# The search for the kept scores of an MoE layer: 16-bit keys in two halves, expert as innermost index

## What is computed

```python
c = einsum('bct,bcd->bdt', x, weights[ids])             # a 32x32 mix per sample
logits = c @ Wg + bg                                     # 4 experts
top_vals, top_idx = top_k(logits, 2); probs = softmax(over the two)
for i in range(4):                                       # capacity = 4096 / 4 = 1024
    score = where(expert i is one of the two, probs[:, i], -inf)
    sel_p, sel_idx = top_k(score, 1024)                  # the kept scores
    y = gelu(c[sel_idx] @ W1[i]) @ W2[i] * p
    out = out.at[sel_idx].add(y)
x = x + out
x = x + ffn(lora_swiglu(x, per-sample adapters))         # second layer
```

## Time and profile before

| | us |
|---|---|
| median of 3 runs | 598.33 |
| lowest, highest | 596.82, 598.34 |
| profiled execution, its own time | 598.46 |
| span of the profile | 596.7 |
| TensorE busy | 569.3 |
| VectorE busy | 380.8 |
| ScalarE busy | 241.0 |
| GpSimd busy | 142.1 |

### The profile page before, as it was taken

One profiled execution on the slowest core, in us unless ns is written; L12 is line 12 of the kernel. 1 busy time (PEld: TensorE's weight loads), 2 busy tenths in 40 slices (PEclk: granted clock), 3 DMA queues, 4 the chain that ended last, 5 costly groups with the idle time before them and its releaser, 6 DMA issues.

```text
span 596.7 us, 10231 instructions
## 1 busy us (share of the span) xinstructions
PE 569.3 (95%) x3548; PEld 474.1 (79%) x3548; DVE 380.8 (64%) x847; ACT 241.0 (40%) x545; POOL 142.1 (24%) x120
## 2 busy tenths in 40 slices
PE   4777899999999999999999999999999999999996
PEld 2656699999999999987878878778788788787885
DVE  6888767875776566656566564575565655744733
ACT  2643347666864754644412422322324033123110
POOL 3000223752563460756003002030030030100000
PEclk9998899999999999999999999999999999999999
DMA  8999579353348331643004105022041041130012
GB/s 301 321 319 291 163 231 332 53 160 74 36 125 282 36 55 18 147 102 88 1 0 131 20 3 137 13 91 55 6 125 24 0 132 18 36 83 8 9 28 35
DMA packets 64653, 61.05 MB, mean 102 GB/s; under 512 B 37504, under 2 KB 56704, under 8 KB 63264
## 3 DMA queue, kind: packets, MB, share of 16 engines
q1 hardware_dynamic: 53168, 37.99, 21.5%
q0 software_dynamic: 9264, 22.22, 15.5%
q10 hardware_dynamic: 2176, 0.26, 0.3%
HBM read 45.19 MB, written 19.47 MB: 108 GB/s over the span
## 4 chain that ended last, share of the span: by engine, by line
PE 88%; DVE 7%; DMA 2%; issue 1%; ACT 1%; SPq 1%; DVEq 0%; ACTq 0%; POOLq 0%
PE bank L1282 25%; PE bank L1283 24%; PE bank L1284 24%; PE bank L1538 5%; PE bank L1496 2%; DMA xT<-in_xT 2%; DVE passed L887 2%; PE bank L1403 1%; PE bank L1488 1%; PE bank L1392 1%; PE bank L1363 1%; PE bank L1505 1%; PE bank L1506 1%; PE bank L1626 1%; PE bank L1586 1%
## 5 line engine op out<-in xcount | busy, mean ns | idle before, releaser
L730 ACT ACTIVATE act<-bank 128x512 f32<-128x512 f32 x64 | 38.2, 599 | 181.4 <-PE bank L1538 181.4
L1238 DVE TENSOR_TENSOR prod<-bank,act 128x512 f32<-128x512 f32 x64 | 44.2, 691 | 93.3 <-PE bank L1538 75.8
L1098 DVE TENSOR_TENSOR hid_lo<-hf,hid_hi 128x512 fp32r<-128x512 f32 (+1 forms) x80 | 46.7, 585 | 51.3 <-ACT hf L660 46.8
L1282 PE MATMUL bank<-w_hi,hid_hi 128*128 128x256 f32 x256 | 71.9, 281 | 0.2 <-DVE hid_lo L1098 0.2
L1283 PE MATMUL bank<-w_lo,hid_hi 128*128 128x256 f32 x256 | 71.4, 279 | 0.0
L1284 PE MATMUL bank<-w_hi,hid_lo 128*128 128x256 f32 x256 | 71.3, 279 | 0.0
L657 ACT ACTIVATE hid_hi<-bank 128x512 fp32r<-128x512 f32 (+1 forms) x80 | 41.1, 514 | 66.1 <-PE bank L1284 59.9
L489 POOL DMA_INDIRECT x_rows<-y_sb,slot_row x32 | 54.5, 1704 | 44.3 <-ACT y_sb L629 33.6
L478 POOL DMA_INDIRECT xg<-flat_rows,slot_row x32 | 34.6, 1082 | 118.5 <-DVE slot_row L953 75.2
L1282 PE MATMUL bank<-xs_hi,w_hi 128*128 128x512 f32 (+1 forms) x160 | 57.5, 360 | 0.1
L508 POOL DMA_INDIRECT b_pair<-b_rows,b_row x8 | 8.3, 1038 | 201.8 <-PE bank L1586 201.2
(11 more groups left out here) (299 smaller groups left out, 1269.5 us busy)
## 6 DMA issues: line engine op xcount, KB each, us to landing
w_raw<-in_L_ffn_W SPq DMA_DIRECT2D x8, 1024.0 KB
flat_rows<-x_sb SPq DMA_DIRECT2D x8, 520.0 KB, 7.2
xT<-in_xT SPq DMA_DIRECT2D x8, 512.0 KB, 8.6
x_sb<-in_x SPq DMA_DIRECT2D x8, 512.0 KB, 8.7
outT<-out_sb SPq DMA_DIRECT2D x120, 32.0 KB
wdT<-in_wdT SPq DMA_DIRECT2D x1, 1024.0 KB, 5.9
wg_lo_raw<-in_L_cond_Wg SPq DMA_DIRECT2D x1, 1024.0 KB, 8.2
wu_lo_raw<-in_L_cond_Wu SPq DMA_DIRECT2D x1, 1024.0 KB
```

The lines of the kernel that those rows point to most:

```text
L730: act.activation(act1[h % 2][:, :], bank[h % 2][:, :], ACT.Silu).then_inc(silu1, 1)
L1098: dve.tensor_tensor(lo[:, n], hf[s % 2][:, n], hi[:, n].bitcast(f32), ALU.subtract).then_inc(hid0, 1)
L1238: dve.tensor_tensor(prod[par][h][:, :], bank[2 + h % 2][:, :], act1[h % 2][:, :], ALU.mult).then_inc(prod1, 1)
L1282: pe.matmul(out, lh, rh, start=start, stop=False, skip_group_check=True)
```

## The change

The pattern is searched in two halves. `high_key` is the score's bits above the lowest 15, `low_key` the lowest 15. In steps 0 to 4 the 16-bit `key` is `high_key`, less 100 for an unused expert; in steps 5 to 9 it is (high_key - found) x 2^15 + low_key, cut to 0 and 2^15 - 1, so that scores outside the found high part compare as all or nothing. Candidates are sums in place of or-ed patterns, the table of step values is fp32 and moves from `pack_i` to `pack_f2`. `key`, `cand` and `passed` have the expert as innermost index. The fp32 `score` is still made, behind the comparisons of step 0, and the threshold is put together from both halves at the end.

```diff
@@ -21,6 +21,7 @@
+HIGH_STEPS, LOW_BITS = 5, 15
@@ -34,8 +35,8 @@
-           "scale": D, "out_bias": KD}
-I_COLS = {"subj": G, "sample": TOK // 32, "steps": SEARCH_STEPS * CAND}
+           "scale": D, "out_bias": KD, "steps": HIGH_STEPS * CAND}
+I_COLS = {"subj": G, "sample": TOK // 32}
@@ -53,15 +54,15 @@
-        "steps": np.broadcast_to(np.concatenate([np.arange(1, CAND + 1, dtype=np.int32) << (SEARCH_BITS * (SEARCH_STEPS - 1 - i))
-                                                 for i in range(SEARCH_STEPS)]), (P, CAND * SEARCH_STEPS)),
+        "steps": np.broadcast_to(np.concatenate([np.arange(1, CAND + 1) * 2.0 ** (SEARCH_BITS * (HIGH_STEPS - 1 - i))
+                                                 for i in range(HIGH_STEPS)]).astype(np.float32), (P, CAND * HIGH_STEPS)),
         "behind": np.broadcast_to(np.repeat(np.arange(E - 1, -1, -1, dtype=np.float32), G), (P, E * G)),
     }
 
 
 def adaln_moe_lora(nc, A, outT):
     f32, f32r, bf16 = mybir.dt.float32, mybir.dt.float32r, mybir.dt.bfloat16
-    i32, u32 = mybir.dt.int32, mybir.dt.uint32
+    i32, u32, i16 = mybir.dt.int32, mybir.dt.uint32, mybir.dt.int16
@@ -107,7 +108,7 @@
-        steps = vi["steps"].bitcast(u32).rearrange("p (i j) -> p i j", j=CAND)
+        steps = vf2["steps"].rearrange("p (i j) -> p i j", j=CAND)
@@ -219,10 +220,12 @@
-        cand = sb("cand", [P, E, CAND], f32)
-        passed = sb("passed", [P, E, CAND, G], bf16)
+        key, cand = sb("key", [P, G, E], i16), sb("cand", [P, CAND, E], i16)
+        passed = sb("passed", [P, CAND, G, E], bf16)
         passed_n = sb("passed_n", [P, E, CAND], f32)
-        kept = [sb(f"kept{i}", [P, E, CAND + 1], f32) for i in range(2)]
+        kept = [[sb(f"kept{i}{j}", [P, E, CAND + 1], f32) for j in range(2)] for i in range(2)]
+        high_key, low_key = sb("high_key", [P, E, G], i32), sb("low_key", [P, E, G], i32)
+        key_f = sb("key_f", [P, 2, G, E], f32)
@@ -233,6 +236,8 @@
+        thr_high, thr_bits = sb("thr_high", [P, E], i32), sb("thr_bits", [P, E], i32)
+        thr = sb("thr", [P, E], f32)
@@ -340,7 +345,7 @@
-        IDLE_STEPS = [2, 2, 2, 2, 2, 4, 8, 8, 8, 8]
+        IDLE_STEPS = [2, 2, 2, 2, 2, 2, 6, 6, 6, 6]
@@ -802,7 +807,8 @@
-            dve.memset(kept[0][:, :, CAND], 0.0)
+            dve.memset(kept[0][0][:, :, CAND], 0.0)
+            dve.memset(kept[1][HIGH_STEPS % 2][:, :, CAND], 0.0)
@@ -875,17 +881,31 @@
-            link(dve.tensor_tensor(score[:, :, :], prob[:, :, :], unused[:, :, :], ALU.subtract))
-
-            counts = bank[7][:, 0:E * CAND * SUMS].rearrange("p (e j g) -> p e j g", e=E, j=CAND)
+            by_e = lambda t: t.rearrange("p e g -> p g e")
+            link(dve.tensor_scalar(high_key[:, :, :].bitcast(u32), prob[:, :, :].bitcast(u32), LOW_BITS, None, ALU.logical_shift_right))
+            dve.tensor_scalar(low_key[:, :, :].bitcast(u32), prob[:, :, :].bitcast(u32), 2 ** LOW_BITS - 1, None, ALU.bitwise_and)
+            link(dve.scalar_tensor_tensor(key[:, :, :], by_e(unused[:, :, :]), -100.0, by_e(high_key[:, :, :]), ALU.mult, ALU.add))
+
+            counts = bank[7][:, 0:E * CAND * SUMS].rearrange("p (j g e) -> p e j g", e=E, j=CAND)
             for i in range(SEARCH_STEPS):
-                now, then = kept[i % 2], kept[(i + 1) % 2]
-                link(dve.tensor_tensor(cand[:, :, :].bitcast(u32), over(now[:, :, CAND].bitcast(u32), CAND),
-                                       steps[:, i, :].unsqueeze(1).to_broadcast([P, E, CAND]), ALU.bitwise_or))
+                high = i < HIGH_STEPS
+                now, then = kept[not high][i % 2], kept[not high][(i + 1) % 2]
+                step = steps[:, i % HIGH_STEPS, :]
+                if i == HIGH_STEPS:
+                    found = kept[0][HIGH_STEPS % 2][:, :, CAND]
+                    link(dve.tensor_tensor(key_f[:, 0, :, :], key[:, :, :], found.unsqueeze(1).to_broadcast([P, G, E]), ALU.subtract))
+                    link(dve.scalar_tensor_tensor(key_f[:, 1, :, :], key_f[:, 0, :, :], 2.0 ** LOW_BITS, by_e(low_key[:, :, :]),
+                                                  ALU.mult, ALU.add))
+                    done(dve.tensor_scalar(key[:, :, :], key_f[:, 1, :, :], 0.0, 2.0 ** LOW_BITS - 1, ALU.max, ALU.min))
+                link(dve.tensor_tensor(cand[:, :, :], now[:, :, CAND].unsqueeze(1).to_broadcast([P, CAND, E]), over(step, E), ALU.add))
                 for g in ASKED:
                     n = g.stop - g.start
-                    dve.tensor_tensor(passed[:, :, :, g], score[:, :, g].unsqueeze(2).to_broadcast([P, E, CAND, n]),
-                                      over(cand[:, :, :], n), ALU.is_ge).then_inc(asked, 1)
+                    dve.tensor_tensor(passed[:, :, g, :], key[:, g, :].unsqueeze(1).to_broadcast([P, CAND, n, E]),
+                                      cand[:, :, :].unsqueeze(2).to_broadcast([P, CAND, n, E]), ALU.is_ge).then_inc(asked, 1)
+                if i == 0:
+                    done(dve.tensor_tensor(score[:, :, :], prob[:, :, :], unused[:, :, :], ALU.subtract))
+                if i == HIGH_STEPS:
+                    done(dve.tensor_scalar(thr_high[:, :], found, 2.0 ** LOW_BITS, None, ALU.mult))
@@ -897,11 +917,14 @@
-                link(dve.scalar_tensor_tensor(now[:, :, 0:CAND], passed_n[:, :, :], float(CAP), cand[:, :, :], ALU.is_ge, ALU.mult))
-                link(dve.tensor_reduce(then[:, :, CAND], now[:, :, :], AX.X, ALU.max))
-            thr = kept[SEARCH_STEPS % 2][:, :, CAND]
-
-            thr_b = over(thr, G)
+                link(dve.scalar_tensor_tensor(now[:, :, 0:CAND], passed_n[:, :, :], float(CAP), cand[:, :, :].rearrange("p j e -> p e j"),
+                                              ALU.is_ge, ALU.mult))
+                if i < SEARCH_STEPS - 1:
+                    link(dve.tensor_reduce(then[:, :, CAND], now[:, :, :], AX.X, ALU.max))
+            link(dve.tensor_reduce(thr_bits[:, :], now[:, :, :], AX.X, ALU.max))
+            link(dve.tensor_tensor(thr[:, :].bitcast(i32), thr_high[:, :], thr_bits[:, :], ALU.bitwise_or))
+
+            thr_b = over(thr[:, :], G)
@@ -1361,7 +1384,7 @@
-                                         passed[:, :, :, g].rearrange("p e j g -> p (e j) g"),
+                                         passed[:, :, g, :].rearrange("p j g e -> p j (g e)"),
```

## The result

The changed kernel takes 596.54 us, the median of 20 executions (595.45 to 598.84), beside 598.43 for 20 of the kernel before on the same chip (596.82 to 599.93). The ratio is 0.9969, 95% interval 0.9960 to 0.9977: 1.9 us faster. The profiled execution took 596.57 us (span 594.7), before 598.46 (596.7).

The account below looks back on a forecast made before the run. The prediction took the front as a latency, the search its largest piece. Savings of 4.45 us less 1.46 added gave 3.0, less 0.4 for the gather 2.6: 595.9 from the profiled 598.46, 595.7 from the median; forecast 595.8, range 594.1 to 598.4.

Parts of the forecast that it names:

- Comparisons at half price: Search step's two comparisons: 0.52 ns per element in place of 1.04, 0.47 us less per step.
- both of its reasons: Comparisons: operands no longer 4-byte data, and no innermost element repeated; together 0.47 us less per step.
- The step: Search steps: five VectorE-bound ones save 0.47 us each, five TensorE-limited ones 0.42, sum 4.45 us.
- The additions: Extra search work: +0.36 ahead of the loop, +0.80 between halves, +0.08 in step 5, +0.22 final OR; sum +1.46 us.
- The net: Search as a whole: 4.45 us saved less 1.46 added, 3.0 us.
- The stores cap at 60.0: Behind the search: flat_rows stores stay down at 60.0, slot rows come at 61.2, so up to 4.2 us gain passes.
- The collision, 0.4 us: First gather at 62.1 meets the load of wu and A matrices: 0 to 1.9 us lost, 0.4 taken.
- No gap downstream, so nothing changes: After the gather: transposes, splits and products move as they are, TensorE has no gap; gain 2.6 us passes.
- a rival only as a gain: TensorE from 65 to 71 us: no collision and full clock, 1.3 us more, 594.3; chance 0.08.
- The sum: Whole kernel: 3.0 us from the search less 0.4 for the gather, gain 2.6 us.
- the first: Rival at the two comparisons: still one element at a time, only additions remain, 599.9 us; chance 0.11.
- The second (gain lost behind the search): Rival: gather held by wu's load, or half clock in more TensorE-bound steps; about 597.2 us; chance 0.16.

Follow-up runs that it names:

- experiment 1: Changed kernel with one comparison condition undone at a time: keys back to fp32 (600.83 us), or 16-bit keys with columns innermost again (600.53 us).
- after_again: The changed kernel, unaltered, run and profiled a second time: 596.50 us, 0.9963 of the kernel before.
- eight_steps: Changed kernel with 8 search steps in place of 10, the threshold lacking its lowest six bits: 595.31 us, 0.9948 of the kernel before.
- the filled kernels: Kernels with eight unread 512-column matmuls in TensorE's wait for the first gather: changed kernel 595.54 us, kernel before 597.77 us.
- experiment 3: Second profile of the changed kernel (596.50 us), and eight unread matmuls in TensorE's gather wait, in the changed kernel (595.54 us) and the one before (597.77 us).
- first_and_filled: Changed kernel with the last flat_rows store ahead of Wg's load and eight unread matmuls in TensorE's gather wait: 595.32 us, 0.9950 of the kernel before.
- loads_late: Changed kernel with the loads of Wu and the two A matrices issued only once the first gathers are in: 596.44 us, 0.9978 of the kernel before.
- no_filler: Changed kernel without the idle matmuls in the search steps: 597.49 us, 0.9993 of the kernel before.
- wait_filled: Changed kernel with eight unread 512-column matmuls in TensorE's wait for the first gather: 595.54 us, 0.9953 of the kernel before.
- before_filled: Kernel before with eight unread 512-column matmuls in TensorE's wait for the first gather: 597.77 us, ratio 0.9985.

## Why the prediction was right

Predicted 595.8 us, range 594.1 to 598.4; measured 596.54, faster. By its steps:

- **Comparisons at half price.** Right: 450 and 326 ns for the 450 and 325 in the text, by both of its reasons (experiment 1). The price today was read a little low: 742 and 501 ns are 1.08 ns per element over 0.14 us, and not 1.04 over 0.15; the 0.47 us come out the same. The Trainium skill's rule ("VectorE: DVE Perf Modes", What auto-detection actually checks) had only half its support in the rows of before; the trace after now agrees with the other half, rows of four included.
- **The step.** Predicted 2.13 and 2.18, measured 2.10 and 2.20; the reduce 1.11 us behind the start, predicted 1.15. The saving: 4.65 us for 4.45, 0.14 of it because two steps of the kernel before were lengthened by the half clock (2.72 us for 2.65).
- **The additions.** 1.67 us for 1.46. Ahead of the loop 29.75 - 28.62 = 1.13 in place of 0.66, so +0.47 for 0.36; between the halves +0.96 for 0.80; 0.05 for 0.08 and 0.19 for 0.22. The mis-sized term is the same in both places: the operations of two sources on 128 elements that make the keys take 0.37 to 0.38 us in the new index order, not the 0.29 of the score. It is the order and not the narrow type: in columns_inner, 16-bit keys in the old order, the same three take 0.28 to 0.29, and in keys_f32, 4-byte keys in the new order, 0.37 to 0.38. The net, 2.98 us, came out at the 3.0 of the text by luck: the two errors, each 0.2, cancel.
- **The stores cap at 60.0.** Right in that nothing was held by them. Wu's load was issued at 60.02 in this profile, but at 57.65 in after_again and at 58.20 in eight_steps, so the 60.0 is no fixed place, and that it came out to 0.02 is luck. No run shows the cap binding.
- **The collision, 0.4 us.** This step failed. The gather did come 0.6 us late, between the bounds, but I followed only the first of two gathers; the second is what TensorE needs last, and it was late by 0.2 at most. So 0.4 us is twice of what it cost, and what the text took off here was taken off elsewhere.
- **No gap downstream, so nothing changes.** I wrote that the chain moves as it is. It does not: its first 3 us now run at half clock. The text had the clock in this stretch as a rival only as a gain (0.79 could rise to 1.00). It went the other way: more of the half level fell on products. That the clock costs this is shown by the filled kernels; that it falls on products because they come earlier is not. There is one unfilled profile of the kernel before, and columns_inner, whose first product came at 72.96, also took 22.46 us. It cost 0.84 us in the profile; the 0.38 us between 2.16 and 2.54 came back behind the second routing, 0.15 of it in TensorE's two waits, the rest within the scatter named in experiment 3.
- **The sum.** From prob to end -2.54 us, predicted -2.6: right in size, by luck: one wrong term (0.4 for the gather) stands in the place of one that was missing (0.84 for the clock, of which 0.38 came back). Against the medians it is 1.9 (1.4 to 2.4 by the interval). prob came at 28.62 in the changed kernel, 29.42 in after_again and 28.08 before; over all profiled kernels it lies between 27.30 and 30.41 with no order by kernel, so one profile each does not say whether the moved tables cost anything at the start. That was not tried by itself, and the difference between 1.9 and 2.5 stays open.

Of the rivals, the first is what keys_f32 and columns_inner show. The second (gain lost behind the search) is right in kind for 0.84 us: the clock, behind the search and not in its steps, and not Wu's load. The best kernel with the full threshold is first_and_filled: 595.32 us, span 592.8 in its profile, not told apart from the changed kernel by interval.

## What to carry to other kernels

A fast form of an instruction is a conjunction of conditions: price the change with each of them missing, since the conversions around it are then a net loss. In the same sum, price the conversions in the order in which they read, not by the plain form. When work is moved forward, read the granted clock at the place it moves to, not only the waits; eight idle matmuls in the wait ahead of the chain that bounds the kernel gave 1.1 us from prob to end (566.08 to 564.95), over a third of what the whole change gave. When a transfer is late, ask which later transfer the consumer waits for anyway, before its delay is charged. Take a second profile of a kernel before a time in it is called a cap or a loss: here two of one kernel differed by 2.4 us in when a load went out and by 0.67 us in one stretch.

## What was not expected of the hardware

- TensorE's granted clock stands at the half level at the start of the expert stage after a wait of 2.53 us for the gather in the changed kernel, of 1.91 in the one before and of 1.92 in loads_late, but at full in no_filler after one of 1.89 us. Of the eleven profiles without filler in the wait, only no_filler has it full there. With eight matmuls in the wait, 0.33 us of it idle, it was full in wait_filled, and also in before_filled and first_and_filled.
- An indirect gather of 0.13 MB issued 2.6 us behind Wu's load took 0.6 us longer to its consumer than without it (3.68 for 3.07), and issued 0.35 us behind it 2.9 us longer (5.98). The Trainium skill ("DMA: Bandwidth & Descriptors", Queues, rings and completion order) has the engines go round their queues packet by packet. The 0.6 us agree with a fair share for a small transfer; the 2.9 us do not, if a packet is taken to be small.
- A two-source operation on 16-bit integers with rows of only four dense elements, and an outer index that repeats, runs at 0.55 ns per element over 0.14 us (450 ns for 560 elements, 326 for 336), and at 1.08 with the innermost index repeated (742 and 501).
- The two-source operations on 128 elements that make the keys took 0.37 to 0.38 us with the expert as innermost index, for 2-byte and for 4-byte keys (changed kernel, keys_f32), and 0.28 to 0.29 with 2-byte keys in the old order (columns_inner).
